# Gated blocks at a fourfold row pitch, norm and bias rows laid out on the host, and the first layer's h as three rounded products behind the third temporal gate

## What is computed

```python
# layer 0: W1, b1, W2, b2, gamma, beta are picked for each batch by its language id
h  = relu(x @ W1[id] + b1[id])                 # 512 -> 128
y  = x + h @ W2[id] + b2[id]                   # 128 -> 512
x1 = x + layernorm(y) * gamma[id] + beta[id]
# layer 1
ctx    = causal_ema(x1, tau_ctx)
gated  = x1 * sigmoid(concat(x1, ctx) @ Wg.T + bg)
mod    = 0.5 + sigmoid(gelu(x1 @ Wn1.T + bn1) @ Wn2.T + bn2)      # 8 values a row
traces = 8 causal EMAs of gated * mod[d]; temporal = their softmax blend
gate   = sigmoid(temporal @ Wtemp.T + btemp)
soma   = gelu(x1 @ Wsoma.T + bsoma)
out    = x1 + layernorm((soma * gate) @ Wout.T) * gamma + beta
```

## Time and profile before

| | |
|---|---|
| median of 3 runs | 1368.03 us (1366.42 to 1370.3) |
| the profiled execution's own time | 1361.66 us |
| its span, first to last instruction | 1359.8 us |
| mean granted TensorE clock | 0.996 |
| PE busy | 1312.5 us (97%) |
| DVE busy | 1028.8 us (76%) |
| ACT, POOL busy | 521.1 us (38%), 373.9 us (28%) |

### The profile page before, as it was taken

One profiled execution on the slowest core, in us unless ns is written; L12 is line 12 of the kernel. 1 busy time (PEld: TensorE's weight loads), 2 busy tenths in 40 slices (PEclk: granted clock), 3 DMA queues, 4 the chain that ended last, 5 costly groups with the idle time before them and its releaser, 6 DMA issues.

```text
span 1359.8 us, 19735 instructions
## 1 busy us (share of the span) xinstructions
PE 1312.5 (97%) x7908; PEld 991.4 (73%) x7908; DVE 1028.8 (76%) x1526; ACT 521.1 (38%) x822; POOL 373.9 (28%) x294
## 2 busy tenths in 40 slices
PE   4889999999999999999999999999999999999997
PEld 2657778677786867768677686777868777786766
DVE  7988677887778777677786768777787786778575
ACT  3425243443524424243343433425244252434422
POOL 4405142051411404133131422304123041421102
PEclk9999999999999999999999999999999999999999
DMA  8382542907247180561706526074451825426060
GB/s 268 130 223 88 156 154 78 240 32 207 103 116 202 70 240 31 149 200 62 218 32 175 174 78 202 32 224 124 117 169 65 232 78 156 154 79 169 36 182 32
DMA packets 91486, 186.25 MB, mean 137 GB/s; under 512 B 9858, under 2 KB 14594, under 8 KB 87298
## 3 DMA queue, kind: packets, MB, share of 16 engines
q1 hardware_dynamic: 82178, 168.20, 42.4%
q10 hardware_dynamic: 9216, 16.78, 3.7%
HBM read 134.61 MB, written 50.33 MB: 136 GB/s over the span
## 4 chain that ended last, share of the span: by engine, by line
PE 36%; DVE 23%; DMA 16%; issue 13%; ACT 6%; SPq 2%; POOL 2%; DVEq 0%; POOLq 0%
PE ring L984 26%; DVE U L863 11%; DMA grep<-g_blocks 8%; DMA g_blocks<-g_f 7%; PE ring L977 4%; SPq L355 2%; DVE x L793 2%; DVE stats L798 2%; ACT U L523 2%; DVE g_f L872 2%; PE Tp L1158 1%; PE Tp L1169 1%; DMA x<-g_blocks 1%; POOL rows L441 1%; PE ring L1183 1%
## 5 line engine op out<-in xcount | busy, mean ns | idle before, releaser
L863 DVE TENSOR_TENSOR U<-grep,w_qs 128x1024 f32<-128x1024 f32 x192 | 227.3, 1219 | 56.9 <-issue 36.7
L412 POOL TENSOR_TENSOR x<-grep,b_row 128x512 f32<-128x512 f32 x64 | 80.5, 1289 | 547.5 <-DMA grep<-in_x 547.5
L1158 PE MATMUL Tp<-U,Arep 128*32 128x256 f32 x2048 | 133.6, 385 | 13.9 <-DVE U L863 13.2
L533 ACT ACTIVATE g_f<-g_f 128x512 f32<-128x512 f32 x64 | 40.4, 632 | 259.3 <-DVE g_f L868 259.1
L425 POOL TENSOR_TENSOR grep<-grep,beta_row 128x512 f32<-128x512 f32 x64 | 82.8, 1327 | 116.7 <-DMA grep<-x_tiles 116.6
L1158 PEld LDWEIGHTS Tp<-U,Arep 128*32 128x32 f32 x2048 | 54.1, 109 | 79.3 <-DVE U L863 39.6
L868 DVE TENSOR_TENSOR g_f<-ring,bg_row 128x512 f32<-128x512 f32 x64 | 44.1, 689 | 85.2 <-PE ring L984 85.2
L984 PE MATMUL ring<-seq_hi,Wtemp_hi 128*128 128x512 f32 x256 | 106.7, 417 | 0.1
L984 PE MATMUL ring<-x1T_hi,Wsoma_hi 128*128 128x512 f32 x256 | 103.2, 403 | 0.0
L984 PE MATMUL ring<-Wg_hi,x1T_hi 128*128 128x512 f32 x256 | 103.2, 403 | 0.0
L984 PE MATMUL ring<-Wout_hi,g_r 128*128 128x512 f32 x256 | 99.8, 390 | 1.1 <-DVE soma_r L720 1.0
(11 more groups left out here) (173 smaller groups left out, 2878.8 us busy)
## 6 DMA issues: line engine op xcount, KB each, us to landing
grep<-g_blocks SPq DMA_DIRECT2D x192, 256.0 KB, 4.5
grep<-in_xc SPq DMA_DIRECT2D x16, 1024.0 KB, 10.8
grep<-in_x SPq DMA_DIRECT2D x16, 1024.0 KB, 9.0
x_tiles<-x SPq DMA_DIRECT2D x16, 1024.0 KB, 9.0
g_blocks<-g_f ACTq DMA_DIRECT2D x64, 256.0 KB, 3.8
x<-g_blocks SPq DMA_DIRECT2D x64, 256.0 KB, 5.3
grep<-x_tiles SPq DMA_DIRECT2D x16, 1024.0 KB, 4.8
out<-U SPq DMA_DIRECT2D x64, 256.0 KB, 2.0
```

The costliest lines, as they stand in the source:

```text
L412: nc.gpsimd.tensor_tensor(new[:, b, :], x_t[:, b, :], b2_row[:, :], ALU.add).then_inc(xb2_ready, 1)
L533: nc.scalar.activation(g[:, b, :], g[:, b, :], ACT.Sigmoid).then_inc(sig_ready, 1)
L863: V_.tensor_tensor(U[:, (n + 2) % 4, :, :], spans_of(k, b)[:, :, at], w_qs[:, hh, at].unsqueeze(1).to_broadcast([P, NI, HC]), ALU.mult).th ...
L1158: last = nc.tensor.matmul(Tp[b % 2][i * L:(i + 1) * L, at], Arep[:, b * NI + i, hh, :], U[:, (n + 2) % 4, i, :], start=(hh == 0 and c == 0 ...
```

## The change

Three edits in the device code, and the host arrays that go with them.

First, `g_dram` gets rows four times as wide, of which the first quarter is used: the block's rows lie 8 KB apart instead of 2 KB, and as many bytes move.

Second, b2, gamma0, beta0, bg, gamma1 and beta1 are repeated 128 times on the host, so that each load reads 128 DRAM rows instead of one row 128 times.

Third, h of tiles 2 to 15 is a split product. ACT rounds W1 and xT, POOL subtracts to get their low parts, at the head of their lists in slots 1 to 14; W1's two parts lie in `Arep`, xT's high part in `U`, its low part in place of xT. PE forms h behind `temporal_gate(2)` instead of `(1)`, and n1 (now `modulation_begun`) stands ahead of y instead of behind it. ACT and DVE take `hidden_high` and `hidden_low` behind `soma_gated(2)`, and ACT's gelu of n1 waits for y, whose operand it overwrites.

In the diff the first block behind the loads is POOL's, the second ACT's, the third PE's.

```diff
-        g_dram = nc.dram_tensor("g_blocks", [NB, P, C], F, kind="Internal").ap()
+        g_dram = nc.dram_tensor("g_blocks", [NB, P, 4 * C], F, kind="Internal").ap()[:, :, 0:C]
...
-                sp.dma_start(b2_row[:, :], b2[bass.ds(one, 1)].to_broadcast([P, C])).then_inc(ld_b2, 16)
+                sp.dma_start(b2_row[:, :], b2[bass.ds(one, 1)].rearrange("a p m -> p (a m)")).then_inc(ld_b2, 16)
...
+                if has_next and k >= 1:
+                    pool.wait_ge(w1hi_ready, k)
+                    nc.gpsimd.tensor_tensor(W1_split[:, 1, :, :], W1[:, :, :], W1_split[:, 0, :, :].bitcast(F),
+                                            ALU.subtract).then_inc(w1lo_ready, 1)
+                    for n in range(NC):
+                        pool.wait_ge(xThi_ready, upto(4, k - 1, n))
+                        nc.gpsimd.tensor_tensor(xT_lo[:, n, :], xT[:, n, :], xT_hi[:, n, :].bitcast(F),
+                                                ALU.subtract).then_inc(xTlo_ready, 1)
...
+                if has_next and k >= 1:
+                    act.wait_ge(full["Uused"], upto(PIECES // 2, k - 1, PIECES // 2 - 1))
+                    if k & 1:
+                        act.wait_ge(ld_w1, 32 * ((k + 1) // 2 + 1))
+                    nc.scalar.activation(W1_split[:, 0, :, :], W1[:, :, :], ACT.Identity).then_inc(w1hi_ready, 1)
+                    act.wait_ge(ld_xT, 16 * upto(1, k + 1, 0))
+                    for n in range(NC):
+                        nc.scalar.activation(xT_hi[:, n, :], xT[:, n, :], ACT.Identity).then_inc(xThi_ready, 1)
...
+                        pe.wait_ge(xThi_ready, upto(4, tile - 2, NC - 1))
+                        for n in range(NC):
+                            nc.tensor.matmul(ps[:, :], W1_split[:, 0, n, :], xT_hi[:, n, :], start=(n == 0), stop=False)
+                        pe.wait_ge(w1lo_ready, tile - 1)
+                        for n in range(NC):
+                            nc.tensor.matmul(ps[:, :], W1_split[:, 1, n, :], xT_hi[:, n, :], start=False, stop=False)
+                        for n in range(NC):
+                            pe.wait_ge(xTlo_ready, upto(4, tile - 2, n))
+                            last = nc.tensor.matmul(ps[:, :], W1_split[:, 0, n, :], xT_lo[:, n, :], start=False,
+                                                    stop=(n == NC - 1))
```

More of the change, by code:

```diff
@@ L100, in cond_resid_kernel @@
         Eend = [sb("Eend_hi", [P, P], R), Eend_lo]
-        grep = [sb(f"grep_{n}", [P, NI, C]) for n in range(2)]
+        grep_1, xT_lo = sb_two_ways("grep_1", [P, NI, C])
+        grep = [sb("grep_0", [P, NI, C]), grep_1]
         x_t = grep[0]
@@ L229, in groups_of @@
             if has_prev:
-                order += [("temp", k - 1, 0), ("temp", k - 1, 1)]
+                order += [("temp", k - 1, e) for e in range(NC - 1)]
             if has_next and k != 0:
@@ L233, in groups_of @@
             if has_prev:
-                order += [("temp", k - 1, 2), ("temp", k - 1, 3)]
+                order += [("temp", k - 1, NC - 1)]
             if has_next:
@@ L293, in load_language @@
                 for row, src in ((gamma0_row, g0), (beta0_row, be0)):
-                    sp.dma_start(row[:, :], src[bass.ds(one, 1)].to_broadcast([P, C])).then_inc(ld_norm, 16)
+                    sp.dma_start(row[:, :], src[bass.ds(one, 1)].rearrange("a p m -> p (a m)")).then_inc(ld_norm, 16)
             def load_split(n, src):
@@ L512, in slot @@
                     act.wait_ge(full["n1"], upto(1, k, 0))
+                    if has_next:
+                        act.wait_ge(full["y"], upto(4, k + 1, NB - 1))
                     nc.scalar.activation(hid[:, :], inner_bank[:, :], ACT.Gelu, bias=col[:, 0:1]).then_inc(h1_ready, 1)
@@ L1044, in slot @@
                 if has_prev:
-                    temporal_gate(0)
-                    temporal_gate(1)
+                    for e in range(NC - 1):
+                        temporal_gate(e)
                 if has_next and k != 0:
@@ L1049, in slot @@
                 if has_prev:
-                    temporal_gate(2)
-                    temporal_gate(3)
+                    temporal_gate(NC - 1)
+                if has_prev and has_cur:
+                    modulation_begun()
                 if has_next:
@@ L1062, in slot @@
                     hidden(1)
-                if has_cur:
-                    pe.wait_ge(ema_ready, upto(4, k, 0))
-                    if k == 0:
-                        pe.wait_ge(split_lo[0], 1)
-                    pe.wait_ge(x1lo_ready, upto(4, k, NC - 1))
-                    split_product(inner_bank[:, :], lambda a, n: Wn1[a][:, n, :], lambda a, n: x1T[a][:, n, :],
-                                  NC).then_inc(full["n1"], 1)
+                if has_cur and not has_prev:
+                    modulation_begun()
                 gated = (soma_hi, soma_lo)
```

44 lines of the change are left out of this document (30 added, 14 removed).

## The result

| | before | after |
|---|---|---|
| median of the timed runs | 1367.22 us (1366.0 to 1370.3, 4 runs) | 1421.63 us (1418.67 to 1426.49, 4 runs) |
| span of the profiled execution | 1359.8 us | 1417.4 us |

The ratio is 1.0398, with a 95% interval of 1.0359 to 1.0436. The change costs 54 us. The forecast of 1358 us was wrong in size and in sign, and the time lies outside its range.

What follows compares the result with a forecast made beforehand. PE's list, played end to end, was taken to bound the kernel. Third edit 9.7 us plus second edit 0.5, first edit 0, gave 10.2 us off the 1368.0 median: 1358 us, range 1344 to 1363.

Steps and rivals of the forecast that it cites:

- I take 0, the end where the destination binds: Block reads: wide rows gain nothing, as 32 partitions a transfer set the rate; other ends 13.2 us faster, 69 us slower.
- the pitch slows the reads: Rival on block reads before products U: a slower block delays PE by nearly its whole lateness; 1374 us, chance 0.07.
- the bound at 118 GB/s: Block reads at the broadcast rows' rate: 8.9 us a block, 4.3 us later in each of 16 slots, 69 us.
- at 1 us a slot: The slower-reads rival's sum: 1368.0 - 10.2 + 16 = 1374 us.
- no row shows any read of separate rows that is slow by its source: Block reads: the argument given against the rival of slower reads, chance 0.07.
- The third edit's 9.7 us: PE's h as twelve f32r matmuls, 2.74 us instead of 3.43: 0.69 us saved in each of 14 slots.
- spare times: Slack to hide the added roundings, subtractions and low part of h on ACT, POOL and DVE: 0.8 to 2 us each.
- Everything that hangs on the first value gate moves 0.69 us ahead together with PE: Sigmoid, g, its store, the reads and U all come 0.69 us earlier, so PE's waits for U stay.
- the idle time of the gate's bias: DVE idles 2.39 us before adding the first value gate's bias; that instruction waits 85.2 us for PE over the kernel.
- POOL's exclusion of DVE: DVE instructions with two SBUF inputs lock against POOL's SBUF reads; taken as 0, by the rule alone 17.5 us.
- One lock of 1.25 us: Worst delay taken for DVE's input norm scaling beside POOL's additions, inside the slack.
- The second edit: Host-repeated rows load faster: 0.5 us gained in the set-up, bounds 0 and 2.

Runs made afterwards that it cites:

- e1: Kernel before with only the g_blocks rows widened to a pitch of 8 KB; 1429.83 us, ratio 1.0478 to before.
- e6: Kernel before plus the third edit alone, with each block's four reads issued in the order 0, 2, 1, 3; 1353.95 us, ratio 0.9917 to before.
- e12: Kernel before plus ScalarE's new order, block reads 0, 2, 1, 3 and GpSimd's set-up wait, without the third edit; 1352.25 us, ratio 0.9885.
- e5: Kernel before plus the third edit, with ScalarE's first soma gelu and a spare one-column Sigmoid ahead of the scalings; 1354.24 us, ratio 0.9925 to before.
- e9: Kernel before plus the third edit, ScalarE's new order, block reads 0, 2, 1, 3 and GpSimd's set-up wait; 1340.23 us, ratio 0.9807.

## Why the prediction was wrong

**The step that failed** is "I take 0, the end where the destination binds", under the first edit, and with it the chance of 0.07 for "the pitch slows the reads". In its place the runs showed 66 us for the first edit alone (e1, 1429.8 - 1363.9). The mechanism was named there, and the bound at 118 GB/s, 69 us, was close to what e1 shows; but that is luck, of two errors that cancel. The rate did not fall to 118: over the reads of the first block e1 moved 166 GB/s, where before had 197. And the bound, like the rival's own "at 1 us a slot", counted one late block in each slot. The four blocks stand behind one another, each store and its reads behind the ones before, and their lateness adds up: the reads of the four blocks land 1.6, 2.8, 3.8 and 4.0 us later in the slot in e1 than before, and the slot got 3.9 us longer. So with the right chance for the rival its time of 1374 would still have been far too low. I weighed the rival by how I explained the rate of the reads and not by the bounds. One end of the term was 69 us away, and the range stopped at 1363. The argument against it, "no row shows any read of separate rows that is slow by its source", was only that no row showed such reads at all. I also spoke of reads alone; the second store, of the same rows, took 5.64 us in place of 4.03 beside the first block's reads, and its own reads wait for it.

**That the destination binds** was half right: e6 shows that the order of neighbouring quarters counts, by 0.3 to 0.4 us of 6.7. It did not follow that the source was free: the same reads became 1.2 us longer by the pitch alone.

**The third edit's 9.7 us.** The sizes were right: h took 2.73 us against 2.74 forecast, nothing waited in gates, h, n1 or y, and ACT's, POOL's and DVE's spare times held. In the kernel's state at the time it was worth 4 us (0.5 to 8.2). The step that failed is "Everything that hangs on the first value gate moves 0.69 us ahead together with PE": the store moved 0.29. Behind the first value gate stood a second releaser, ACT's scalings and its table load, 0.28 us behind the first in before (the sigmoid began at 637.24, the logits ended at 636.96), and then DVE's turn against POOL, which was the later of the two: in e12 the sigmoid alone came earlier, and the store did not. I had read the idle time of the gate's bias, the 85.2 us in the earlier trace rows, and taken it for the whole chain. e5, e9 and e12 settle it: with both out of the way, and the reads shorter, the edit brings 11 to 12 us.

**POOL's exclusion of DVE.** I priced it at 0 on the places that I had looked at, and no wait of PE in before or after shows a cost there. It did cost where I had not looked: on DVE's multiplication before the first store, in every slot, and in the set-up. One lock of 1.25 us was no bound either: in one slot of e6, W2's low part took 12.60 us. The rule of the Trainium skill that I had quoted, page "SBUF — State Buffer", section "Who interferes with whom", agrees with the trace in both (1.41 us in place of 0.69, 1.22 in place of 0.15); that rule and a row agreed did not say which instruction it would meet.

**The second edit**: 0.5 us forecast, with bounds of 0 and 2; measured as a ratio of 1.0015 (0.9988 to 1.0042), which is no gain that can be told from none. **The set-up**: 6 us by which the profiled execution of before lay under its median was named as a difference, not explained. A set-up that ends at 105.2 us in place of 111 or so is of that size. No trace of a slower run of before is there to show it, but the granted clocks of the 60 runs of before beside the experiments point there: the three at 0.996 or 0.997, like the profiled one (0.996), took 1357 us in the mean, the 34 at 0.991 or less 1367, and in the traces it is in the set-up that the clock is low.

## What to carry to other kernels

A buffer in DRAM that is written and read back in rows should have dense rows, or a pitch a little off the power of two (256 bytes were nearly enough here). An unknown cost whose bounds are 69 us apart needs a range that spans them or one look before it is called 0, and lateness in a chain of transfers is counted once for each link. Before a us taken out of the bounding engine's list is counted, follow the first thing that leaves it (here a store) back over all of its releasers, and ask how far behind the first the second one is. When two gains fail to add up, try them on each other: here the third edit brought 4 us alone and 11 to 12 behind three small ones.

## What the hardware showed that I had not expected

- Rows of 2 KB at a pitch of 8192 bytes: the second store of a slot 5.64 us against 4.03, reads of a block of 1 MB 7.9 to 11.0 us against 6.7 to 7.7; at 8448 bytes 4.36 and 7.1 to 8.6. The DMA engines are busy for less of the time while it happens (0.70 against 0.82 over the first block's reads), the middle packet is quicker (84 against 153 ns), and 10% of the packets take over 300 ns, against 1.4%.
- A DVE operation of one column takes 1.22 us instead of 0.15 beside POOL's additions, and the first store of a slot is timed by the end of a POOL instruction. Once, a subtraction of 1.5 us was held for 12.60 us behind POOL's additions.
- Four reads of one block into four groups of 32 partitions are 0.3 to 0.4 us faster in the order 0, 2, 1, 3 than in the order 0, 1, 2, 3.
